# Block attention on one Trainium2 core: TensorE issues a quad's scores first, then three turns, the values, the results' turn and the fourth turn; VectorE copies the fourth turn a quad later

## The reference, cut to what matters

```
scores = einsum("bihd,bjhd->bhij", q, k) * d ** (-0.5)
scores = where(mask, scores, NEG)
p = softmax(scores, axis=-1)
o = einsum("bhij,bjhd->bihd", p, v)
o = o * rsqrt(mean(o * o) + EPS) * o_norm_w      # then @ Wo.T
```

## Time and profile before

| | us |
|---|---|
| median of 3 runs | 669.48 (669.45 to 670.17) |
| the profiled execution, its own time | 669.69 |
| its span, first to last instruction | 667.9 |
| TensorE busy | 647.5 (97% of the span) |
| VectorE busy | 500.6 (75%) |
| ScalarE busy | 404.0 (60%) |
| GpSimd busy | 292.8 (44%) |

### The profile page before, as it was taken

How to read it: one execution, slowest core, us unless ns; L and a number is a source line. 1 busy time by engine, 2 the same in 40 slices (tenths; PEclk the granted TensorE clock), 3 DMA queues, 4 the chain that set the end, 5 groups by cost and what they waited for, 6 DMA issues and landing times.

```text
span 667.9 us, 13616 instructions
## 1 busy us (share of the span) xinstructions
PE 647.5 (97%) x4692; PEld 565.9 (85%) x4692; DVE 500.6 (75%) x1428; ACT 404.0 (60%) x1057; POOL 292.8 (44%) x268
## 2 busy tenths in 40 slices
PE   5999999999999999998999998999999999999998
PEld 3777888898989889897888866666899999999997
DVE  6797876878787787867688997998677745645545
ACT  3766148788888888888965369888553222222221
POOL 1584246455465647363234619993523700400000
DMA  8902034544455353435390011002000000000000
GB/s 316 379 2 102 2 113 116 158 142 152 126 163 169 113 185 96 136 117 151 128 371 3 0 33 80 3 2 92 38 1 1 1 17 1 1 17 1 1 18 16
DMA packets 26884, 59.52 MB, mean 89 GB/s; under 512 B 3178, under 2 KB 12780, under 8 KB 26432
## 3 DMA queue, kind: packets, MB, share of 16 engines
q1 hardware_dynamic: 23744, 50.45, 22.8%
q0 software_dynamic: 3072, 8.20, 3.7%
HBM read 48.34 MB, written 10.49 MB: 88 GB/s over the span
## 4 chain that ended last, share of the span: by engine, by line
PE 72%; DVE 18%; ACT 6%; issue 3%; DMA 0%; POOL 0%; DVEq 0%; ACTq 0%
PE bank L2343 10%; PE bank L2081 8%; PE bank L2015 7%; PE bank L2072 6%; PE bank L2394 5%; PE bank L2368 5%; PE bank L2101 4%; PE bank L2092 4%; PE bank L2022 4%; PE bank L2143 3%; ACT sb L1202 3%; PE bank L2410 3%; PE bank L2312 2%; PE bank L1955 2%; PE bank L2297 2%
## 5 line engine op out<-in xcount | busy, mean ns | idle before, releaser
L1076 ACT ACTIVATE sb<-bank,sb 128x256 f32<-128x256 f32 x128 | 59.6, 472 | 39.1 <-DVE sb L1562 33.8
L1265 ACT ACTIVATE h_parts<-sb 128x256 fp32r<-128x256 f32 x56 | 23.4, 418 | 76.5 <-DVE sb L1852 45.7
L2081 PE MATMUL bank<-sb 128*128 128x256 f32 x256 | 66.2, 381 | 0.0
L1562 DVE TENSOR_REDUCE sb<-bank 128x2 f32<-128x512 f32 x64 | 43.6, 682 | 28.5 <-PE bank L2081 28.0
L2343 PE MATMUL bank<-rounded,b_lo 128*128 128x256 f32 x224 | 62.9, 281 | 0.0
L2343 PE MATMUL bank<-rounded,b_hi 128*128 128x256 f32 x224 | 62.8, 281 | 0.0
L2343 PE MATMUL bank<-am_lo,b_hi 128*128 128x256 f32 x224 | 62.8, 280 | 0.0
L832 POOL DMA_INDIRECT expert_out<-sb x32 | 32.8, 1026 | 57.4 <-DVE sb L1504 44.0
L1083 ACT ACTIVATE sb<-sb 128x256 f32<-128x256 f32 x128 | 57.8, 504 | 0.1
L1843 DVE TENSOR_TENSOR sb<-sb,bank 128x256 f32<-128x256 f32 x56 | 23.4, 418 | 44.5 <-ACT sb L1226 44.3
L1226 ACT ACTIVATE sb<-bank 128x256 f32<-128x256 f32 x56 | 21.4, 382 | 53.1 <-PE bank L2343 53.1
(11 more groups left out here) (336 smaller groups left out, 1920.2 us busy)
## 6 DMA issues: line engine op xcount, KB each, us to landing
sb<-in_w_gate_up SPq DMA_DIRECT2D x32, 368.0 KB
sb<-in_w_down SPq DMA_DIRECT2D x32, 256.0 KB
sb<-in_w_pair SPq DMA_DIRECT2D x8, 704.0 KB
expert_out<-sb SPq DMA_DIRECT2D x1, 4096.0 KB, 22.8
sb<-expert_out SPq DMA_DIRECT2D x8, 512.0 KB, 7.0
sb<-in_w SPq DMA_DIRECT2D x1, 1792.0 KB, 13.0
sb<-in_b SPq DMA_DIRECT2D x1, 1792.0 KB, 7.6
sb<-in_sw_up SPq DMA_DIRECT2D x1, 1536.0 KB, 9.0
```

What stands on the lines that cost most here:

```text
L1076: act.activation(probs[:, u % 4, q, :], bank[3 + u % 2][:, q * S:(q + 1) * S], ACT.Exp, scale=-1.0, bias=row_min[:, u % 4, q:q + 1], accum ...
L1562: dve.tensor_reduce(row_min[:, u % 4, :], bank[3 + u % 2][:, :].rearrange("p (q n) -> p q n", q=QT), AX.X, ALU.min).then_inc(at_min, 1)
L2081: mm = pe.matmul(bank[3 + u % 2][:, q * S:(q + 1) * S], qb[i][:, h, b * S + q * P:b * S + (q + 1) * P], keys[:, h, b * S:(b + 1) * S], sta ...
```

## The change

TensorE's loop now starts with the scores of quad Q, where two turns of the quad before used to come first; then come three turns in a row, the values, the results' turn, and last the fourth turn. VectorE's copy of that fourth turn moves to the head of its next loop. No instruction is added or taken away, and no wait is written differently.

```
--- VectorE
             for Q in range(QUADS + 4):
+                if 1 < Q <= QUADS + 1:
+                    odd_probsT(4 * Q - 5)
                 if Q > 3:
                     heads_out(Q - 4)
                 if 2 < Q < QUADS + 3:
                     quad_out(Q - 3)
                 if Q == QUADS + 2:
                     gated(0, 0)
-                if 0 < Q <= QUADS:
-                    odd_probsT(4 * Q - 3)
                 if Q == 0:
                     first_minima()
                 elif Q < QUADS:
                     masked_minimum(4 * Q)
                     masked_minimum(4 * Q + 1)
                 if 0 < Q <= QUADS:
-                    odd_probsT(4 * Q - 1)
+                    odd_probsT(4 * Q - 3)
                 if 0 < Q < QUADS:
                     masked_minimum(4 * Q + 2)
                     masked_minimum(4 * Q + 3)
--- TensorE
             for Q in range(QUADS + 3):
-                if 0 < Q <= QUADS:
-                    probs1_turn(4 * Q - 4)
-                    probs1_turn(4 * Q - 3)
                 if Q < QUADS:
                     scores1(Q)
                 if Q == QUADS:
                     hidden1(0)
                 if 0 < Q <= QUADS:
+                    probs1_turn(4 * Q - 4)
+                if 0 < Q <= QUADS:
+                    probs1_turn(4 * Q - 3)
                     probs1_turn(4 * Q - 2)
-                    probs1_turn(4 * Q - 1)
...
                     values1(Q - 2)
                 if Q > 2:
                     quad_turn(Q - 3)
+                if 0 < Q <= QUADS:
+                    probs1_turn(4 * Q - 1)
                 if Q == QUADS + 1:
                     hidden1(1)
```

## The result

The changed kernel takes 670.62 us (22 runs) against 669.47 for the kernel before (22 runs): ratio 1.0018, 95% interval 1.0012 to 1.0024. It is slower by 1.15 us, or 0.18%. The forecast was 3.2 us slower: the direction was right, the size was about a third of it. The 1.15 us also lie under the 1.3 us that the prediction itself had named as the least that can be told from no change; that they can be told here is owed to 22 runs of each kernel.

What follows compares the result with a forecast made beforehand. No engine was full; a loop of waits through TensorE, VectorE and ScalarE set 4.21 us a quad. Beginning, middle and end summed as -0.90 + 11 x 0.19 + 2.05 = +3.2 us, forecasting 672.7, range 670.2 to 675.0.

Steps and rivals of the forecast that it cites:

- The loop that is removed: Waits through scores, VectorE's minima, ScalarE's exponents and a turn back to the next scores; sum 4.21 us, the whole old period.
- The bank's round trip: Third turn waits for the first turn and ScalarE's copy of bank 5: 0.56 + 0.47 + 0.15 = 1.18 us, uncovered.
- The distance from the bf16 part to the first turn: TensorE's gap within a quad, read as 0.50 us with a copy's wait suspected; taken as 0.40, ends 0.35 and 0.50.
- The coupling of the two loops: TensorE's queue at 4.40 us a quad against VectorE's loop from the fourth turn at 4.28; TensorE's sets the pace.
- Two mechanisms, each enough alone to lose what was gained: TensorE's queue, 4.40 us a quad, and VectorE's loop from the fourth turn, 4.28, both over the old 4.21.
- The beginning: Start of the stage up to scores 4, reached at 413.83 against 414.73: a gain of 0.90 us, once.
- The middle: Scores 4 to scores 15: 11 periods of 4.40 us, each 0.19 longer than before.
- The end: Scores 15 to the last values: 11.69 us against 9.64, +2.05, from two turns, the bank's trip and a longer wait.
- The rest: After the stage TensorE is busy 167.19 of 168.00 us, so gains or losses carry to the kernel's end nearly whole.
- the rival of no difference: Weight load ahead of the copy's end and shortest gap after the bf16 part: 4.21 to 4.24 a quad, 670.3; chance 0.13.
- the hidden tail: Rival: the feed-forward swallows the 2 us lost at the end; +1.2, 670.7; chance within that of the rival of no difference.

Runs made afterwards that it cites:

- first copy in three: Changed kernel with ScalarE's copy of each quad's first turn (unit 4Q-4) made in three pieces of 128 columns; 672.22 us, ratio 1.0034 to the kernel before.
- third behind values: Changed kernel with one line moved, the third turn (4Q-2) placed behind the values; 667.60 us, ratio 0.9963 to the kernel before.

## Why the prediction was wrong

- **The loop that is removed.** Right: its sum of 4.21 was the period, and its waits are gone.
- **The bank's round trip.** Right in place and size: 1.17 against 1.18, nothing covers it (what the first copy in three adds arrives whole), and its wait goes if the values stand in between (third behind values).
- **The distance from the bf16 part to the first turn. This is the step that failed.** The prediction said "I take 0.40, ends 0.35 and 0.50"; it is 0.24. I had seen that 0.50 held a wait, and had a row in which f32 matmuls started before the bf16 ones had ended, giving 0.33, and still put the low end above it. The value lay outside both ends. 0.16 of a quad's 4.40 is this term; 0.04 more is the fourth turn's 0.42 for 0.45 and the round trip's 1.17 for 1.18, and 0.03 came back through the coupling below: 4.23. The ends of the whole period were mis-added besides: from the ends that the prediction states for its terms the sum is 4.32 to 4.53, not 4.30 to 4.57; the measured 4.23 lies under either.
- **The coupling of the two loops.** The prediction had both, 4.40 and 4.28, and let the larger set the pace. The second is no loop of one quad: what counts is half of the two quads' path, 8.47, so with TensorE's at 4.20 the periods alternate and 4.235 is the mean. By the prediction's own terms it would have been 3.95 + 4.73 = 8.68, 4.34 a quad, under 4.40, so there this cost nothing. "Two mechanisms, each enough alone to lose what was gained" holds: the changed kernel has 4.20 and 4.27 where 4.21 was removed.
- **The beginning.** Right: -0.90 was forecast up to scores 4, measured is 16.83 - 17.78 = -0.95. The third turn of the second loop starts at 407.81 behind ScalarE's copy, 407.75 before, as the prediction said.
- **The middle.** Eleven periods of 4.40 were to be 2.1 us longer; they are 46.56 against 46.34, 0.22 longer. This 1.9 us is nearly all of the miss.
- **The end.** +2.05 forecast, +1.74 measured. The whole difference lies in front of `hidden1(0)`, which starts 4.10 after scores 15 and not 4.40: 0.20 is the shorter quad, and 0.1 that it starts 0.33 behind the fourth turn and not 0.45. The chain behind it, up to the last values, is as forecast.
- **The rest.** "Carried to the end of the kernel nearly whole": to 0.02 us.

With 0.24 in place of 0.40 the same sum gives -0.90 + 11 x 0.03 + 1.89 = +1.3, against +1.0 in the profiles and +1.15 in the runs. The range, 670.2 to 675.0, holds the measured 670.62 only because it took in a part of the rival of no difference (+0.3 to +1.3); the low ends of the forecast's own terms give +2.0, 671.5. Of the mechanisms this rival came nearest, by its second condition alone, the short distance behind the bf16 part; its first, a weight load ahead of the copy's end, did not occur. The time given for the hidden tail, 670.7, is nearer still, but that is luck: the tail was not hidden, its 1.74 us arrived whole. The Trainium skill, TensorE: Matmul & The Clock Gate, What happens when you issue a matmul, says that weight loads can be pulled ahead of running matmuls. The trace agrees at the place where I had not applied it (the first turn's load begins 0.22 before the bf16 matmuls end) and not across a wait.

## What to carry to other kernels

A distance that ends right after another engine's release, at the same interval as a known wait, can be a wait even where the profile writes "issue", as it was here; take it out of the sum whole, and let the low end of what is left reach the nearest row. When a loop of waits is broken by reordering, list the pairs that share a buffer and see what now stands between them: here two turns into one bank had the scores between them and then only one other turn, and one line moved turned 1.0018 into 0.9963. Price the last pass of such a loop by itself: an order that is neutral in the middle cost 1.7 us where the pipeline runs out.

## What the runs showed of the hardware

- Three f32 transposes behind four bf16 matmuls start 0.23 to 0.24 us after the first of these, 0.16 before the last ends by the profile's model.
- A ScalarE copy of 384 columns out of PSUM in one piece and in three of 128 differ by only 0.13 us in all in the changed kernel (0.49 and 0.62) and by 0.10 in the kernel before (0.47 and 0.57). I had estimated 0.3 to 0.6.
- A loop of waits of 4.20 us a quad and a path of 8.47 us over two quads that share the scores gave periods of 4.20 and 4.26 in strict alternation over ten quads, a single period of 4.32 when the first was made longer by 0.12 to 0.13, and a single one of 4.19 to 4.20 when the second was made shorter.
- Behind a wait of 0.34 us on ScalarE's copy, TensorE's weight load started 0.12 us after the copy's end and its matmul 0.03 us after the load.
